# Distance attention: position products written to PSUM without gaps, and ACT's copies reading PSUM with a step

## The chip, the cores and the metric

The kernel runs on one core of a Trainium2 chip. The metric is the device time of one execution in microseconds (us). A core has five engines that run side by side and meet through semaphores: TensorE (PE in the profile; PEld is its weight load), VectorE (DVE), ScalarE (ACT), GpSimd (POOL) and SyncE (SP), which here issues DMAs. PE writes its results to PSUM; DVE and ACT read them from there.

## The reference

Four layers run one after the other on x of shape (8, 512, 128): a sine-weighted attention, a mixture of experts, distance attention, and a mixture of experts again. The change is in the third. Cut to that layer (16 heads of 8 values, sequence length 512, of which the positions' table is clamped at its ends):

```python
q, k, v = [(h @ W.T + b).reshape(B, S, 16, 8) for each of q, k, v]
scores = einsum('bqhd,bkhd->bhqk', q, k) / sqrt(8)           # content
pos_emb = dist_emb[MAX_POS - 1 + (pos_q[:, None] - pos_q[None, :])]
scores = scores + einsum('bqhd,qkd->bhqk', q, pos_emb)       # r1: the query with the distance
scores = scores + einsum('bkhd,qkd->bhqk', k, pos_emb)       # r2: the key with the distance
probs  = softmax(scores, axis=-1)
ctx    = einsum('bhqk,bkhd->bqhd', probs, v)
x      = x + ctx
```

## The kernel before

`distance_attention` works in 64 units. A unit u is one query block q of 128 positions of two batches (16 of them, 32 heads together, BH = 32) with one of QT = 4 key tiles of 128 positions. Four units, kt = 0 to 3, make a query block. The unit with kt = 0 of the next query block is the turn: in it the finished block is also transposed, exponentiated and multiplied with V.

One list `plan` sets the order of PE, ACT and DVE alike. A plain unit (kt = 1, 2, 3) is four steps "r1", four steps "r2", four steps "c". In the turn, 16 steps "e" (turn the scores), 8 steps "pv" (values) and 2 steps "o" (outputs) stand between them: r1 x4, r2 x2, e, e, r2, e, e, pv, r2, and so on.

Every step but "pv" fills a slot of `psR`, a ring of RING = 3 slots of two PSUM banks (1024 FP32 values per partition). A fill may start when the fill three places before it in the plan has been taken (`free_slot`): r1, r2 and e are taken by ACT, c and o by DVE.

- **Products** (`positions`, L1709): the position products of a step are 16 matmuls. Each loads a 112 x 128 window of the table `T` as weights, shifted by two positions from one matmul to the next, and moves 64 columns of `qb` (r1) or `kb` (r2): two positions n, 32 heads h. A bank takes 8 matmuls, so 16 positions of 32 heads.
- **Copies** (`keep`, L1785): ACT copies the 1024 values of a slot into `r1` or `r2` in SBUF, both laid out as [128, head, position].
- **Content** (`content`, L1721 and L1724): 8 matmuls of q with k for 8 heads, gapless output, then 8 transposes of `r1` that add to the same place. The first of a unit waits until ACT has copied the last r1 step.
- **Adds** (L1822): DVE adds the slot and `r2` into `S`. The first of a unit waits until ACT has copied the last r2 step. Then four maxima over `S` (L1830); in the turn also the maximum over the key tiles (L1834) and the subtraction for every head (L1837).
- **Spreading** (`spread`, L1655): POOL lays ks out as `kb` for every unit, and qs as `qb` once in a query block, in two copies each, after SP has loaded them (L1610). `load_k(u)` waits until the content of unit u - 2 is done. In the unit with kt = 2 POOL spreads ks, then qs for the next query block, and only then ks of the next unit.

Of the kernel before, what the change touches and what calls it, by code (L numbers as in the profile page):

```python
# [1510 lines left out]
def distance_attention(nc, sb, ps, sem, a, X, ident, dram):  # L1511
# [5 lines left out]
    BH = NB * H  # L1517
# [4 lines left out]
    CP = P // CH  # L1522
    HB = BH // 4
    NPAIR = BH // 2
    RING = 3
# [39 lines left out]
    with ExitStack() as c:  # L1565
# [15 lines left out]
        psR = ps(c, "psR", [P, RING, 2, L])  # L1581
# [11 lines left out]
        act_took = sem(c, "act_took")  # L1593
# [87 lines left out]
        def _(pe):  # L1681

            def free_slot(n):
                if n >= RING:
                    old = fills[n - RING]
                    if old in by_act:
                        pe.wait_ge(act_took, by_act[old])
                    else:
                        pe.wait_ge(dve_took, by_dve[old])
                return psR[:, n % RING, :, :]  # L1690

            def positions(kind, u, k):
                q, kt = divmod(u, QT)
                qt = q % QT
                if kind == "r1":
                    src, way, w0 = qb[:, q % 2, :, :, :], 1, L - 1 + P * kt - P * qt
                    if k == 0:
                        pe.wait_ge(qb_ready, 2 * (q + 1))
                else:
                    src, way, w0 = kb[:, u % 2, :, :, :], 0, L - 1 + P * qt - P * kt  # L1700
                    if k == 0:
                        pe.wait_ge(kb_ready, 2 * (u + 1))
                n = fill[kind, u, k]
                slot = free_slot(n)
                for j in range(CP // 2):
                    pair = k * (CP // 2) + j
                    w = w0 - 2 * pair
                    out = slot[:, j // 8, :].rearrange("p (h n) -> p n h", h=BH)
                    mm = pe.matmul(out[:, 2 * (j % 8):2 * (j % 8) + 2, :], T[:, way, w:w + P],  # L1709
                                   src[:, pair, :, :], start=(j % 8 == 0), stop=True,  # L1710
                                   skip_group_check=True)
                mm.then_inc(filled, 1)
# [51 lines left out]
            for kind, i, k in plan:  # L1764
                if kind in ("r1", "r2"):
                    positions(kind, i, k)
                elif kind == "c":
                    content(i, k)
                elif kind == "e":
                    turn(i, k)  # L1770
                elif kind == "pv":
                    values(i, k)
                else:
                    outputs(i, k)

        @block.scalar
        def _(act):

            def keep(kind, u, k):
                n = fill[kind, u, k]  # L1780
                act.wait_ge(filled, n + 1)
                if kind == "r2" and u:
                    act.wait_ge(dve_took, by_dve["c", u - 1, 3])
                dst = r1 if kind == "r1" else r2
                act.copy(dst[:, :, k * CP:(k + 1) * CP].rearrange("p h (a n) -> p a h n", a=2),  # L1785
                         psR[:, n % RING, :, :].rearrange("p a (h n) -> p a h n", h=BH)).then_inc(act_took, 1)

            def weigh(q, j):
                n = fill["e", q, j]
                act.wait_ge(filled, n + 1)  # L1790
                pair = q * NPAIR + j
                if pair >= RING_W:
                    act.wait_ge(pv, (pair - RING_W) // 2 + 1)
                act.activation(W[:, pair % RING_W, :, :].rearrange("p a n -> p (a n)"),  # L1794
                               psR[:, n % RING, :, :].rearrange("p a n -> p (a n)"),
                               ACT.Exp, scale=1.0 / SHARP).then_inc(act_took, 1)

            def take(q, i):
                if q or i:
                    act.wait_ge(filled, fill["o", q - (i == 0), 1 - i] + 1)  # L1800
                act.wait_ge(pv, q * NQUAD + (i + 1) * GPB)
                act.copy(oS[:], psO[:, i, :, :].rearrange("p g n -> p (g n)")).then_inc(o_taken, 1)

            for kind, i, k in plan:
                if kind in ("r1", "r2"):
                    keep(kind, i, k)
                elif kind == "e":
                    weigh(i, k)
                elif kind == "pv" and k % GPB == GPB - 1:
                    take(i, k // GPB)  # L1810
# [108 lines left out]
```

## Time and profile before

| | us |
|---|---|
| median of 3 runs | 4286.14 |
| lowest, highest | 4275.76, 4294.15 |
| the profiled execution | 4281.09 |
| its span, first to last instruction | 4279.3 |

A profile is one execution. Its span is 1.8 us shorter than that execution's time. Its page shows in 40 slices of 107 us how busy each engine was, and which share of its full clock PE was granted; there are two levels, 2.4 GHz (1.0) and 1.2 GHz (0.5), and a slice shows their mean. The timeline shows instructions in order of time, merged into groups; "idle before" is what the engine waited for. The ends of matmuls are modelled, their starts are recorded; a matmul lasts far longer than the distance to the next one's start, since they are pipelined. So the pace of PE is read from starts.

### The profile page before, as it was taken

To read this page: it belongs to the slowest core of one execution; us is meant where nothing else is said; L and a number is where in the kernel's file an instruction comes from. 1 tells how busy PE (TensorE), PEld (TensorE's weight loads), DVE (VectorE), ACT (ScalarE), POOL (GpSimd) and SP (SyncE) were. 2 spreads that over 40 slices of the span, in tenths; PEclk is the share of its full clock that TensorE was granted. 3 is DMA by queue.
4 is the path that set the end of the run, shared out by engine and by line. 5 is a ranking of instruction groups with operands and counts; after the bars stand their busy time and mean duration, and the time that the engine had idled before them with its cause. 6 is when DMAs were issued, how large, how long until landed. Compare 5 with 4: busy or idle time off the path is not lost. (4 is left out here: it accounts for less than half of the span.)

```text
span 4279.3 us, 71834 instructions
## 1 busy us (share of the span) xinstructions
PE 3602.2 (84%) x27092; PEld 2304.4 (54%) x27092; DVE 3409.0 (80%) x4519; ACT 2868.0 (67%) x2433; POOL 1271.6 (30%) x918
## 2 busy tenths in 40 slices
PE   3799999999999999999658814999999999998890
PEld 2233333333333333333347814989989889987690
DVE  6899999999999999999465544777777777776662
ACT  3899999999999999999323313555565565654430
POOL 2111111112112121212003343544544544531245
PEclk8899999999999999999869957999999999998895
DMA  5000000000000000000221227222223223312022
GB/s 141 17 12 6 12 12 12 6 12 12 12 9 9 12 12 12 6 12 9 99 71 36 61 65 164 54 47 59 55 45 59 55 45 59 61 31 80 20 64 67
DMA packets 149707, 174.78 MB, mean 41 GB/s; under 512 B 63824, under 2 KB 124848, under 8 KB 141264
## 3 DMA queue, kind: packets, MB, share of 16 engines
q1 hardware_dynamic: 140752, 153.35, 15.5%
q0 software_dynamic: 8704, 17.84, 1.8%
q8 instruction: 186, 3.05, 0.3%
q14 instruction: 65, 0.53, 0.0%
HBM read 119.04 MB, written 52.10 MB: 40 GB/s over the span
## 5 line engine op out<-in xcount | busy, mean ns | idle before, releaser
L704 PE MATMUL psA<-wave,diag 128*128 128x512 f32 x3072 | 1445.5, 622 | 136.5 <-DVE score L860 86.7
L772 ACT ACTIVATE wave<-wave 128x2048 f32<-128x2048 int32 x640 | 1181.2, 1904 | 3.6 <-DVE wave L847 2.2
L704 PEld LDWEIGHTS psA<-wave,diag 128*128 128x128 f32 x3072 | 584.4, 197 | 897.5 <-issue 699.2
L1785 ACT COPY r<-psR 128x1024 f32<-128x1024 f32 x512 | 482.6, 1039 | 358.1 <-PE psR L1709 357.5
L641 POOL TENSOR_TENSOR diag<-ident,par 128x128 f32<-128x128 f32 x384 | 292.6, 788 | 1441.0 <-PE psA L704 1441.0
L1655 POOL COPY kb<-ks 48x2048 bf16<-48x2048 bf16 x128 | 486.4, 3800 | 638.2 <-DMA ks<-kb_parts 534.5
L822 DVE TENSOR_SCALAR wave<-s,par 128x2048 int32<-128x2048 int32 x480 | 612.1, 1275 | 0.0
L847 DVE TENSOR_SCALAR wave<-wave 128x2048 int32<-128x2048 int32 x512 | 609.3, 1215 | 0.0
L1822 DVE TENSOR_TENSOR S<-psR,r 128x1024 f32<-128x1024 f32 x256 | 313.5, 1225 | 290.1 <-PE psR L1724 272.0
L737 ACT ACTIVATE s<-psS,par 128x1024 int32<-128x1024 f32 x256 | 282.8, 1105 | 132.4 <-PE psS L667 132.4
L1794 ACT ACTIVATE W<-psR 128x1024 f32<-128x1024 f32 x256 | 252.2, 1040 | 150.7 <-PE psR L1733 150.7
L860 DVE SCALAR_TENSOR_TENSOR score<-wave,par,psA 128x1024 f32<-128x1024 f32 x256 | 317.7, 1272 | 39.2 <-PE psA L704 39.2
L860 DVE SCALAR_TENSOR_TENSOR score<-wave,par,score 128x1024 f32<-128x1024 f32 x256 | 316.4, 1275 | 0.0
L1733 PE MATMUL psR<-ident,S 128*128 128x128 f32 x2048 | 269.5, 289 | 48.6 <-DVE S L1837 47.6
L1837 DVE TENSOR_SCALAR S<-S,m 128x512 f32<-128x512 f32 x512 | 307.8, 674 | 2.3
L1830 DVE TENSOR_REDUCE mx<-S 128x8 f32<-128x1024 f32 x256 | 297.8, 1210 | 0.0
L1709 PE MATMUL psR<-qb,T 112*128 112x64 bf16 x4096 | 244.5, 248 | 41.3 <-POOL qb L1655 41.3
L1733 PEld LDWEIGHTS psR<-ident,S 128*128 128x128 f32 x2048 | 241.5, 149 | 66.7 <-DVE S L1837 56.5
L1724 PE MATMUL psR<-ident,r 128*128 128x128 f32 x2048 | 266.8, 273 | 0.0
L1709 PEld LDWEIGHTS psR<-qb,T 112*128 112x128 bf16 x4096 | 237.0, 126 | 45.1 <-issue 42.1
L1709 PE MATMUL psR<-kb,T 112*128 112x64 bf16 x4096 | 245.8, 247 | 17.2 <-POOL kb L1655 17.2
L1709 PEld LDWEIGHTS psR<-kb,T 112*128 112x128 bf16 x4096 | 233.5, 125 | 23.3 <-POOL kb L1655 19.9
(254 smaller groups left out, 4473.7 us busy)
## 6 DMA issues: line engine op xcount, KB each, us to landing
ks<-kb_parts SPq DMA_DIRECT2D x128, 384.0 KB, 5.9
qs<-qb_parts SPq DMA_DIRECT2D x32, 384.0 KB, 8.5
ys<-f_ys SPq DMA_DIRECT2D x36, 256.0 KB
wave_out<-og SPq DMA_DIRECT2D x33, 256.0 KB, 2.1
o<-wave_out SPq DMA_DIRECT2D x8, 1024.0 KB, 5.1
qp<-qa_parts SPq DMA_DIRECT2D x32, 192.0 KB, 3.5
kp<-ka_parts SPq DMA_DIRECT2D x32, 192.0 KB, 4.0
f_wu<-in_w_up SPq DMA_DIRECT2D x2, 2048.0 KB, 10.4
```

The lines of the kernel that those rows point to most:

```text
L704: mm = pe.matmul(psA[:, kt, :], diag[:, h % 2, f, :], wave[:, h % 2, f, kt * L:(kt + 1) * L], start=(f == 0), stop=(f == PE_F - 1), skip_g ...
L772: act.activation(wave[:, h % 2, f, :], angle[:, h % 2, f, :], ACT.Sin, scale=float(TWO_PI / 2.0 ** 32)).then_inc(sine, 1)
L822: dve.tensor_scalar(angle[:, h % 2, f, :], src, scalar, par[:, u, row, h * NF + f:h * NF + f + 1], ALU.mult, ALU.add).then_inc(turned if f ...
L847: dve.tensor_scalar(angle[:, h % 2, f - 1, :], at, 32 - FRAC, None, ALU.logical_shift_left).then_inc(cut, 1)
L860: dve.scalar_tensor_tensor(out=score[:, u * HG + h, cols], in0=wave[:, h % 2, f, cols], scalar=par[:, u, 1, h * NF + f:h * NF + f + 1], in ...
L1655: pool.tensor_copy(dst[rows, :, odd, :], src[rows, :, :].rearrange("r h (n two) -> r n h two", two=2)[:, :, :, odd]).then_inc(ready, 1)
L1709: mm = pe.matmul(out[:, 2 * (j % 8):2 * (j % 8) + 2, :], T[:, way, w:w + P], src[:, pair, :, :], start=(j % 8 == 0), stop=True, skip_group ...
L1733: mm = pe.matmul(slot[:, i, kt * P:(kt + 1) * P], S[:, 2 * j + i, kt * P:(kt + 1) * P], ident[:], start=(kt == 0), stop=True, is_transpose ...
L1785: act.copy(dst[:, :, k * CP:(k + 1) * CP].rearrange("p h (a n) -> p a h n", a=2), psR[:, n % RING, :, :].rearrange("p a (h n) -> p a h n", ...
L1822: dve.tensor_tensor(S[:, hs, kt * P:(kt + 1) * P], psR[:, n % RING, :, :].rearrange("p a (h n) -> p (a h) n", n=P), r2[:, hs, :], ALU.add) ...
L1830: dve.tensor_reduce(mx[:, hs, kt], S[:, hs, kt * P:(kt + 1) * P], AX.X, ALU.max).then_inc(maxed, 1)
L1837: dve.tensor_scalar(S[:, h, :], S[:, h, :], m[:, h:h + 1], None, ALU.subtract).then_inc(shifted, 1)
```

## The change

Two access patterns change, and with them the place of each value inside a PSUM slot. Before, a bank held [head, position]: value (h, n) lay at 16 h + n, and the 64 results of a product went to 32 places 64 bytes apart, two neighbours each. Now a bank holds [position, head]: value (n, h) lies at 32 n + h, and the 64 results lie in one row. ACT read a slot in order and wrote to SBUF in runs of 16 values. Now it reads with a step of 32 values (128 bytes) through both banks, 32 positions for each head, and writes runs of 32. The values in `r1` and `r2` are the same. The number and order of instructions on every engine and all waits stay as they are.

```diff
-                    out = slot[:, j // 8, :].rearrange("p (h n) -> p n h", h=BH)
+                    out = slot[:, j // 8, :].rearrange("p (n h) -> p n h", h=BH)
                     mm = pe.matmul(out[:, 2 * (j % 8):2 * (j % 8) + 2, :], T[:, way, w:w + P],
                                    src[:, pair, :, :], start=(j % 8 == 0), stop=True,
                                    skip_group_check=True)
...
-                act.copy(dst[:, :, k * CP:(k + 1) * CP].rearrange("p h (a n) -> p a h n", a=2),
-                         psR[:, n % RING, :, :].rearrange("p a (h n) -> p a h n", h=BH)).then_inc(act_took, 1)
+                act.copy(dst[:, :, k * CP:(k + 1) * CP],
+                         psR[:, n % RING, :, :].rearrange("p a (n h) -> p h (a n)", h=BH)).then_inc(act_took, 1)
```

## Rows read from the trace of the kernel before

**Rows 1.** The page, part 2: PE's busy tenths and its clock, 40 slices.
```profile
PE   3799999999999999999658814999999999998890
...
PEclk8899999999999999999869957999999999998895
```
**Rows 2.** Timeline of a plain unit: start, us, engine, line, operation, [idle before <-releaser].
```profile
2912.01 3.74 PE L1709 MATMUL psR<-qb,T 112*128 112x64 bf16 x64
...
2913.10 7.43 ACT L1785 COPY r<-psR 128x1024 f32<-128x1024 f32 x8 [5.05 <-PE psR L1709]
...
2915.55 3.76 PE L1709 MATMUL psR<-kb,T 112*128 112x64 bf16 x64
...
2920.48 0.61 PE L1721 MATMUL psR<-ks,qs 112*128 112x128 bf16 x8
...
2920.68 5.20 DVE L1822 TENSOR_TENSOR S<-psR,r 128x1024 f32<-128x1024 f32 x4 [2.75 <-PE psR L1724]
...
2920.93 1.04 PE L1724 MATMUL psR<-ident,r 128*128 128x128 f32 x8
...
2924.46 3.74 PE L1709 MATMUL psR<-qb,T 112*128 112x64 bf16 x64
```
**Rows 3.** Instructions by line: duration in ns, min/median/max, first and last start.
```profile
L1709 PEld LDWEIGHTS psR<-kb,T x4096: 96/126/126, 2649.1 to 3887.2; 112*128 112x128 bf16 x196
...
L1785 ACT COPY r<-psR x512: 1012/1030/1094, 2643.7 to 3887.6; 128x1024 f32<-128x1024 f32 x171
...
L1655 POOL COPY kb<-ks x128: 3659/3810/3992, 2641.7 to 3878.7; 48x2048 bf16<-48x2048 bf16 x128
```
**Rows 4.** Timeline: first unit's start, POOL's copies, third unit, turn, next start.
```profile
2899.39 3.84 PE L1709 MATMUL psR<-qb,T 112*128 112x64 bf16 x63
...
2905.87 7.69 POOL L1655 COPY kb<-ks 48x2048 bf16<-48x2048 bf16 x2 [32.81 <-DMA ks<-kb_parts]
...
2929.08 3.75 PE L1709 MATMUL psR<-kb,T 112*128 112x64 bf16 x64 [0.88 <-POOL kb L1655]
...
2937.97 3.74 PE L1709 MATMUL psR<-qb,T 112*128 112x64 bf16 x64
...
2944.57 7.62 POOL L1655 COPY kb<-ks 48x2048 bf16<-48x2048 bf16 x2 [5.24 <-DMA ks<-kb_parts]
...
2945.42 9.43 DVE L1837 TENSOR_SCALAR S<-S,m 128x512 f32<-128x512 f32 x8
...
2952.53 1.97 PE L1733 MATMUL psR<-ident,S 128*128 128x128 f32 x16 [2.64 <-DVE S L1837]
...
2977.15 3.06 PE L1709 MATMUL psR<-qb,T 112*128 112x64 bf16 x49
```
**Rows 5.** Waits, 2641 to 3890 us: waiting <- awaited, us, times, longest.
```profile
PEld psR L1709 <- POOL kb L1655: 19.9, 16, 2.2
```
**Rows 6.** Instructions by line, as rows 3: DVE's reads of PSUM.
```profile
L977 DVE TENSOR_SCALAR orec<-psG x8: 224/225/226, 2102.0 to 2149.8; 128x64 f32<-128x64 f32 x8
L989 DVE TENSOR_TENSOR Y<-psY,bo x32: 278/280/293, 2107.2 to 2155.6; 128x128 f32 x32
L1329 DVE COPY f_ys<-f_pp x36: 678/681/692, 2321.7 to 4181.8; 128x512 f32<-128x512 f32 x36
```
**Rows 7.** Timeline: the r1 products of the first unit, at half clock.
```profile
2641.76 6.48 PE L1709 MATMUL psR<-qb,T 112*128 112x64 bf16 x64 [41.27 <-POOL qb L1655]
```
**Rows 8.** Stretches: length, busy us of the engines, PEclk, DMA share, GB/s.
```profile
2709.00:2712.40 3.40, 1.38 (x26) 1.06 (x18) 3.40 (x2) 1.78 (x2) 2.90 (x1) 1.00 0.00 0
2712.40:2715.80 3.40, 3.40 (x20) 3.07 (x23) 3.37 (x8) 1.03 (x1) 0.00 (x0) 0.50 0.00 0
...
2777.20:2819.50 42.30, 39.15 (x588) 35.15 (x586) 31.09 (x49) 24.13 (x26) 8.58 (x3) 0.92 0.21 39
2858.30:2899.50 41.20, 37.98 (x589) 34.69 (x587) 31.18 (x49) 24.13 (x26) 8.94 (x3) 0.96 0.21 40
2938.00:2977.20 39.20, 36.56 (x588) 33.27 (x586) 30.55 (x49) 24.02 (x26) 8.89 (x3) 1.00 0.21 42
```

## The prediction

> **What bounds the kernel now.** I read the page first for the stages [rows 1]. The change touches only distance attention, slices 25 to 37 of 40, 2641.8 to about 3893 us. There PE is busy in nine tenths of nearly every slice, at nine tenths of its clock. Busy shares don't say who sets the pace, so I went to the timeline of a plain unit [rows 2]. One (query block, key tile) unit is 12.45 us long, from PE's r1 products at 2912.01 to the next at 2924.46. PE has no gap: 64 r1 products (3.55 us), 64 r2 products (3.57), four content blocks of 1.33 each (5.3). ACT's eight copies begin 1.09 us after the first product and follow each other every 0.91 us ((7.43 - 1.03) / 7, with the 1.03 of one copy from rows 3). PE fills a slot in 16 x 56 ns = 0.90 us. So in the product phase PE and ACT have one pace; the content phase is PE's alone. DVE's first add waits for the last copy (2920.53, add at 2920.68).
>
> The third unit of each query block and the turn differ [rows 4]. POOL spreads ks(2), qs and ks(3) in one row, from 2905.87 until 2929.0, and PE's r2 products wait for it (0.88 us; there are 16 such waits, of 15 third units and the first unit of all, up to 2.2 us [rows 5]). In the turn, PE waits 2.64 us at 2952.53 for DVE's subtraction of the maximum. Eight of those subtractions take 9.43 us, and the wait ends when POOL's copy of 2944.57 to 2952.19 is over. Both waits belong to POOL and to the landing of ks, which this change doesn't touch.
>
> **Part 1: the products.** Each of 8192 products reads 64 columns and writes 64 values per partition, 64 bytes apart, two by two. They start 56 ns apart: 64 of them from 2912.01 to 2915.55 [rows 2]. The content matmuls, 128 columns with an equally large weight load and a gapless output, also start 56 ns apart: eight from 2920.48 to 2920.93. So a product takes as long as a matmul of twice its columns. Is that the strided write or the weight load? The load of a product takes 126 ns in the median but 96 at the least [rows 3]: most wait some 30 ns for something, and a load that finds the array free isn't the limit. That leaves the write, or a floor for changing weights. Bounds for the new interval: below, 27 ns (half of 55, the columns alone); above, 56 (no change). I take 30, near the lower end, since content shows that load and matmul overlap fully; at 40 the sum changes by 0.15 us a unit. A slot is then filled in 0.48 us.
>
> **Part 2: the copies.** 512 copies read 1024 values at 128-byte steps. No row shows ACT reading with a step. The nearest is DVE at L977, 64 values of PSUM at the same 128-byte step, 225 ns [rows 6]. Gapless reads of PSUM by DVE give (681 - 280) / (512 - 128) = 1.04 ns a value, so 64 would take 280 - 64 x 1.04 = 213. The step costs at most 12 ns on 64 values, 0.19 ns each; on a copy that is 0 to 0.2 us. I take 0. That the runs it writes get longer I cost at nothing: at 0.91 us for 1024 values ACT already takes 0.89 ns a value, less than the 1.04 of those gapless reads.
> The Trainium skill, "Advanced Engine Details and Errata", section Memory Cachelines, says that PSUM lines hold two FP32 values and that every two consecutive elements should be contiguous. That speaks for the faster product and against the copy; if it held for ACT's reads as for PE's writes, the third rival below would be the result. The DVE row doesn't bear it out for reads.
>
> **Part 3: a plain unit, step by step** (t from the first product). First copy at 0.48 + 0.2 = 0.70 instead of 0.90 + 0.2 = 1.09. Copies are then ACT's own, every 0.90. PE runs ahead, but the ring has three slots: content block 0 takes the slot of the sixth copy, free at 0.70 + 5 x 0.90 + 1.02 + 0.1 = 6.3. Then 5.3 of content: the unit is 11.64 instead of 12.45, 0.81 less. So of 128 x 26 ns = 3.3 us that PE saves, ACT's pace eats 2.5. DVE's adds fit in: the first waits for the eighth copy (8.2), later ones follow the content blocks, and the last ends 1.4 after the unit, as now (1.5).
>
> **Part 4: what POOL keeps.** From the start of the first unit after a turn (2899.39), POOL's row ends 29.7 us later whatever PE does: 6.5 until ks has landed, 23.2 for six copies [rows 4]. Units 1 and 2 gain 1.5 together, and PE only waits longer in unit 3: r1 is done 2.6 after its start at 23.6 (11.95, since the first of these units waits for DVE's adds, + 11.64), then PE idles some 3.5 us. From the end of that wait, the unit took 8.85 (3.57 + 5.3) and now takes 0.70 + 0.90 + 1.02 + 0.1 + 5.3 = 8.0. So a query block gains 0.85, not 2.4. In the turn, the end of POOL's copy sets when PE goes on, 14.6 us in; behind it PE has 24.6 us of work without a product in it. The turn gains the 0.1 of DVE's last add. Sum: 15 query blocks x 0.85 = 12.8, the last, without a qs to spread, 2.3, first unit 0.85 (its r2 waits for POOL too, rows 5), turns 1.5: **-17.4 us**.
>
> **Part 5: the clock.** PE's waits grow, and waits cost clock here [rows 8]. A stretch with 1.38 us of PE in 3.4 is followed by one at 0.50; the turn whose 2.6 us wait stands in rows 4 kept 1.00. The granted clock was 1.00 in that turn of 39.2 us, 0.96 in one of 41.2, 0.92 in one of 42.3; these three stand for the 15. Cut out the same way, 4 of the 15 turns are of the first kind, 6 of the second, 5 of the third (mean 41.0). With the new products the work ahead of the wait is done some 1.4 us sooner, so the wait becomes 4.0 us; I take no turn to keep the clock, 9 at 41.2 and 6 at 42.4, mean 41.7: **+11 us** (bounds 0 and +21, all at 42.4). In unit 3 the wait of 3.5 us is new: a stretch of 3.4 us at half clock behind it lies partly over products that ACT paces anyway and partly over content, where it costs up to 1.7. I take 0.6, the nearer end being that of the products: **+9** (bounds 0 and +26).
>
> Sum: -17.4 + 11 + 9 = +2.6. The profiled execution took 4281.1 us (span 4279.3), 5 below the median 4286.1 of the runs shown, so 4283.7 against the one and 4288.7 against the other: I say **4286**. This case alone spans 4264 (no cost of clock) to 4316 (both upper bounds).
>
> **Rivals.**
> 1. The interval stays at 56 ns, because changing weights has a floor and not the write. For it: at half clock the 64 first products took 6.48 us [rows 7] instead of 3.74, so the limit scales with PE's clock, as a floor in the array would. Against: content overlaps load and matmul in the same 56. Then nothing moves: 4281 to 4286.
> 2. Slower: PE's clock falls in the product phases of every unit, not only behind the long waits. Now PE has no gap there [rows 2]; after, it works 0.48 and waits 0.42 in each 0.90. Against it: the waits are short, and the turn of rows 4 kept its clock over one of 2.64. No row shows so fine a pattern of work and waits, and it decides as soon as the chip takes it as it took the waits of the other turns. Price: one stretch of 3.4 us at half clock on content in each of 64 units, 64 x 1.7 = 109, less the 17: 4373. The Trainium skill, "TensorE: Matmul & The Clock Gate", section HAM oscillation, tells of a kernel that loses the clock in every round to a wait; that is this rival's course.
> 3. Slower: ACT reads stepped values at half rate, a copy every 1.81 us. A unit is then 0.7 + 5 x 1.81 + 1.9 + 0.1 + 5.3 = 17.05, three of them 51.2 instead of 38.6, x 16 = +201; the turn resumes at 17.5 instead of 14.6, x 15 = +45: 4527. It decides from about 1.1 us a copy; below that POOL's waits hide it.
> 4. Faster: the clock holds in the waits and POOL's copies get shorter, toward their shortest, 3.66 instead of 3.81 [rows 3]: six in a row give 0.9 a query block, -14 beyond the -17: 4250.
>
> **Chances.** Forecast 0.53; rival 1 0.18; rival 2 0.10; rival 3 0.12; rival 4 0.07. A measurement of this kernel can tell about 0.5%, 21 us, from no change (4265 to 4308). The forecast lies inside that bound by 0.39, above it by 0.09, below by 0.05; rival 1 inside by 0.17, and 0.01 above. Faster 0.05 + 0.06 = 0.11; same 0.39 + 0.17 + 0.01 (rival 4) = 0.57; slower 0.09 + 0.01 + 0.10 + 0.12 = 0.32. The range leaves out rival 3, part of rival 4 and the end of rival 2: 4260 to 4360.
>
> **What would show each step.** Part 1: 64 products of r1 in about 2.5 us or ring-bound, weight loads near 98 ns in the median. Part 2: L1785 at 1.01 to 1.03 us, 0.90 apart. Part 3: plain units of 11.6. Part 4: r2 of the third unit still ending a wait for POOL, now about 3.5 us, the three units together 37.7 instead of 38.6. Part 5: 0.50 stretches behind the waits, about 15 and up to 15 more; PE's clock 1.00 in the product phases. The prediction is wrong if L1785 grows past 1.1 us, if the loads stay at 126, or if the mean clock of the stage falls below about 0.95.

## The result and the profile after

| | before | after |
|---|---|---|
| median, us (11 runs each) | 4283.54 | 4299.68 |
| lowest, highest | 4273.48, 4294.15 | 4289.86, 4308.77 |
| span of the profiled execution | 4279.3 | 4300.5 |

The ratio of after to before is 1.0037, with a 95% interval of 1.0024 to 1.0050: the change makes the kernel 16 us slower. The forecast was 4286, a step of +2.6. What moved is read in the order of the prediction.

**The products are twice as fast, the copies as fast as before.** By line (duration in ns, min/median/max, first and last start), as [rows 3]:

```profile
L1709 PEld LDWEIGHTS psR<-kb,T x4096: 96/99/134, 2654.4 to 3908.7; 112*128 112x128 bf16 x196
L1709 PE MATMUL psR<-kb,T x4096: 189/193/242, 2654.4 to 3908.7; 112*128 112x64 bf16 x196
L1785 ACT COPY r<-psR x512: 1012/1030/1099, 2648.0 to 3909.9; 128x1024 f32<-128x1024 f32 x171
```

The load of a product fell from 126 to 99 ns in the median, about what the content's loads take (98 ns, before and after). The copies kept 1012/1030, although each now reads PSUM with a step of 128 bytes.

**A plain unit, the third unit and the wait in the turn.** PE's timeline (start, us, ..., what it waited for), to be held against [rows 2] and [rows 4]:

```profile
2918.18 1.10 PE L1709 MATMUL psR<-qb,T 112*128 112x64 bf16 x32
2919.66 1.11 PE L1709 MATMUL psR<-qb,T 112*128 112x64 bf16 x32 [0.38 <-DVE S L1822]
2920.92 0.63 PE L1709 MATMUL psR<-kb,T 112*128 112x64 bf16 x16 [0.15 <-ACT r L1785]
2921.74 0.64 PE L1709 MATMUL psR<-kb,T 112*128 112x64 bf16 x16 [0.20 <-ACT r L1785]
2922.66 0.64 PE L1709 MATMUL psR<-kb,T 112*128 112x64 bf16 x16 [0.28 <-ACT r L1785]
...
2924.59 0.61 PE L1721 MATMUL psR<-ks,qs 112*128 112x128 bf16 x8 [0.36 <-ACT r L1785]
...
2929.89 1.10 PE L1709 MATMUL psR<-qb,T 112*128 112x64 bf16 x32
2931.38 1.11 PE L1709 MATMUL psR<-qb,T 112*128 112x64 bf16 x32 [0.39 <-DVE S L1822]
2935.98 3.48 PE L1709 MATMUL psR<-kb,T 112*128 112x64 bf16 x64 [3.50 <-POOL kb L1655]
2939.29 0.61 PE L1721 MATMUL psR<-ks,qs 112*128 112x128 bf16 x8
...
2944.60 1.10 PE L1709 MATMUL psR<-qb,T 112*128 112x64 bf16 x32
...
2954.84 0.64 PE L1709 MATMUL psR<-kb,T 112*128 112x64 bf16 x16
2959.67 3.61 PE L1733 MATMUL psR<-ident,S 128*128 128x128 f32 x16 [4.19 <-DVE S L1837]
```

Sixteen products take 0.63 us, of which the last one's own 0.19 is not interval: (0.63 - 0.19) / 15 = 29 ns between starts, where it was 56. But from 2921.74 on the slots follow each other at 0.92 us, ACT's pace, and PE waits 0.2 to 0.3 us for each. The unit is 2929.89 - 2918.18 = 11.71 us instead of 12.45. In the third unit PE now waits 3.50 us for POOL (2935.98; 3.67 in the mean of the 14 middle query blocks, where it was 1.05), and the next turn begins at 2944.60. In the turn it waits 4.19 us for the subtraction (2959.67); the longest wait of a turn is 3.85 us in the mean of the 15, where it was 2.93.

**The clock.** Stretches of this kernel (length, busy us of PE, PEld, DVE, ACT, POOL, PEclk, DMA share, GB/s). The first row is the second half of a turn and, from 2906.3 on, two plain units and a third unit up to the last 0.3 us of its wait. Then come 5.8 us of another third unit (r1 products and all but the last 0.6 us of the wait for POOL), and what follows them; then the wait in a turn, and what follows it:

```profile
2884.70:2935.70 51.00, 43.98 (x792) 40.01 (x792) 35.50 (x44) 29.59 (x32) 22.62 (x6) 1.00 0.25 48
2848.00:2853.80 5.80, 2.50 (x69) 2.25 (x67) 5.70 (x6) 3.76 (x4) 5.74 (x2) 1.00 0.63 137
2853.90:2860.70 6.80, 6.34 (x84) 6.28 (x85) 0.47 (x2) 3.76 (x4) 5.90 (x3) 0.50 0.02 4
2955.20:2959.60 4.40, 0.28 (x10) 0.16 (x6) 4.40 (x3) 1.27 (x2) 4.07 (x2) 1.00 0.00 0
2959.70:2963.10 3.40, 3.40 (x16) 3.24 (x16) 3.40 (x7) 1.03 (x1) 0.00 (x0) 0.50 0.02 5
```

And the same view over 1160 us of the stage, kernel before:

```profile
2680.00:3840.00 1160.00, 1098.71 (x16812) 1039.88 (x16811) 872.17 (x1087) 678.41 (x728) 556.00 (x147) 0.98 0.27 52
```

kernel after:

```profile
2680.00:3840.00 1160.00, 972.94 (x16592) 888.92 (x16592) 849.93 (x1052) 666.78 (x716) 553.06 (x146) 0.93 0.27 52
```

The time in it at half clock rose from 55 to 167 us, in 11 stretches before and 29 after. Before, all lay in turns (11 of the 15). After, over the whole layer, one begins in the wait for POOL, mostly near its end, in each of the 15 third units that have such a wait, and one lies in 14 of the 15 turns. In the product phases of the first and second units, with their waits of 0.2 to 0.4 us, the clock stayed at 1.00 in all query blocks but one. There ks had landed late, and PE waited 1.28 us for POOL in the second unit too; the clock fell behind that wait, and the unit took 12.60 us instead of 11.71:

```profile
3324.83 3.57 PE L1709 MATMUL psR<-kb,T 112*128 112x64 bf16 x64 [1.28 <-POOL kb L1655]
...
3324.90:3328.30 3.40, 3.40 (x65) 3.40 (x66) 2.00 (x2) 2.91 (x4) 3.40 (x1) 0.50 0.41 67
```

To see where the time went, the lengths of the units, from start to start of their r1 products, in us, as means over the 14 query blocks in the middle. All kernels of the experiments stand in it:

| | turn | first | second | third |
|---|---|---|---|---|
| before | 41.04 | 12.62 | 12.45 | 13.68 |
| after | 41.41 | 11.85 | 11.78 | 15.91 |
| fill3 | 41.66 | 11.85 | 11.71 | 14.44 |
| fill_both | 39.69 | 11.85 | 11.71 | 14.20 |
| qturn_before | 38.60 | 12.62 | 12.45 | 12.45 |
| qturn_after | 39.41 | 11.85 | 11.71 | 11.71 |
| poolturn_before | 36.59 | 12.62 | 12.45 | 12.45 |
| poolturn_after | 35.97 | 11.87 | 11.71 | 11.71 |
| act_only | 40.93 | 12.62 | 12.45 | 13.74 |
| step2 | 40.95 | 12.62 | 12.45 | 13.55 |
| pairs | 40.67 | 13.32 | 13.25 | 13.25 |
| read_step | 40.24 | 13.32 | 13.25 | 13.25 |
| pairs_write | 41.71 | 11.87 | 11.71 | 15.79 |

A query block of after is 80.95 us long, of before 79.79: 1.16 more, times 15 is 17 us. The first two units give 1.44 back, the third takes 2.23, the turn 0.37.

### The profile page after: what moved, and what is told of

Same layout as the page of the kernel before. It is cut to its first block and busy times, and to the rows that moved or that the text cites. A ratio compares the mean times of both kernels' runs of the same rounds, so it can differ in the third digit from the quotient of the medians.

```text
span 4300.5 us, 71834 instructions
## 1 busy us (share of the span) xinstructions
PE 3474.3 (81%) x27092; PEld 2148.8 (50%) x27092; DVE 3406.5 (79%) x4519; ACT 2867.9 (67%) x2433; POOL 1271.9 (30%) x918
## 5 line engine op out<-in xcount | busy, mean ns | idle before, releaser
L1724 PE MATMUL psR<-ident,r 128*128 128x128 f32 x2048 | 276.3, 279 | 0.0
L1709 PE MATMUL psR<-kb,T 112*128 112x64 bf16 x4096 | 180.4, 206 | 97.2 <-POOL kb L1655 62.6
L754 ACT ACTIVATE score<-score 128x2048 f32<-128x2048 f32 x132 | 241.4, 1899 | 6.1 <-DVE score L860 5.7
L679 PE MATMUL psO<-score,Vg 128*9 128x512 f32 x1056 | 239.8, 596 | 6.8 <-ACT score L754 6.8
L1724 PEld LDWEIGHTS psR<-ident,r 128*128 128x128 f32 x2048 | 228.9, 145 | 0.0
```

What stands on the lines that cost most here:

```text
L1724: mm = pe.matmul(slot[:, j, :], r1[:, k * HB + j, :], ident[:], start=False, stop=True, is_transpose=True, skip_group_check=True)
```

## Experiments

The theory: the 1.44 us that the first two units save in a query block are lost to POOL's row of copies in any case, and the time on top comes from half clock behind the two longer waits. The rivals: the new access patterns themselves cost something (ACT's stepped reads, or more traffic in the third unit), or the turn is what got slower for a reason of its own. Kernels that ran beside each other share the runs of before. These had medians of 4288.4, 4254.2 and 4254.5 us in the three groups, so times are compared within a group, and between groups by ratio alone.

### Filling the third unit's wait (fill3)

Kernel after, with 50 matmuls that nobody reads in place of part of PE's wait for POOL. What they write is overwritten by the products.

```diff
                     if k == 0:
+                        if kt == 3 and q < NQ - 1:
+                            busy = free_slot(fill[kind, u, k])
+                            for j in range(50):
+                                pe.matmul(busy[:, 0, 0:P], T[:, 0, 0:P], T[:, 0, P:2 * P],
+                                          start=True, stop=True, skip_group_check=True)
                         pe.wait_ge(kb_ready, 2 * (u + 1))
```

> The changed kernel, with 50 matmuls of 128 columns (56 ns each, 2.8 us) that PE does into the free slot while it waits for POOL's kb in the third unit of the first 15 query blocks. Their results are overwritten; every wait and every other instruction stays. Theory (the loss is the granted clock that falls behind that wait of 3.5 to 4.3 us): the third unit goes from 15.9 us to 13.7 to 14.2, units 1 and 2 stay at 11.85 and 11.71, the stretch at half clock around the third unit goes away, the turn stays at 41.4: 15 x 1.9 = 28 us less than the changed kernel, near 4271, ratio to the kernel before 0.997. Rival (the wait itself, or POOL's and the DMAs' pace, costs the time, and the clock is only seen beside it): the third unit stays at 15.9 and the time at 4300.

Measured: 4282.38 us (12 runs) beside 4288.41, ratio 0.9983 (0.9970 to 0.9996). PE's timeline in the third unit, the filler at L1705 and products now at L1714:

```profile
2852.34 2.97 PE L1705 MATMUL psR<-T 112*128 112x128 bf16 x50
2855.91 1.57 PE L1714 MATMUL psR<-kb,T 112*128 112x64 bf16 x48 [0.60 <-POOL kb L1655]
...
2858.65 0.61 PE L1726 MATMUL psR<-ks,qs 112*128 112x128 bf16 x8 [0.36 <-ACT r L1790]
```

The stretches around it, which answer to 2848.00 and 2853.90 of after:

```profile
2851.10:2855.90 4.80, 4.07 (x82) 3.78 (x82) 4.52 (x5) 3.02 (x4) 4.69 (x2) 1.00 0.74 143
2855.90:2863.90 8.00, 7.46 (x128) 7.22 (x129) 3.42 (x3) 3.76 (x4) 7.11 (x2) 1.00 0.01 3
```

PE is no earlier at its products: POOL's row ends 29.84 us after the first unit's start, against 29.89 in after and 29.86 in before (means). What changed is the time from there to the next turn: 8.16 us instead of 9.64 (before: 8.89), and 8.05 in most query blocks. So more work on PE makes this kernel 0.54% faster than after (1.0037 to 0.9983, across groups), some 23 us, and 15 times the third unit's 1.47 is 22. Neither ACT's reads nor PE's writes changed in it, so neither is the cause in the third unit. The third unit came out at 14.44 us, a little above the 13.7 to 14.2 expected: POOL's row ends 6.28 us into that unit, and 8.05 us follow even at full clock, 14.33 in all.

### Filling both waits (fill_both)

fill3, and 55 more ahead of the turn's long wait.

```diff
             def turn(q, j):
+                if j == 4 and q < NQ - 1:
+                    busy = free_slot(fill["e", q, j])
+                    for i in range(55):
+                        pe.matmul(busy[:, 0, 0:P], T[:, 0, 0:P], T[:, 0, P:2 * P],
+                                  start=True, stop=True, skip_group_check=True)
                 pe.wait_ge(shifted, q * BH + 2 * j + 2)
```

> The changed kernel with the 50 matmuls in the third unit's wait for POOL, and 55 more (3.1 us) that PE does in the turn's wait of 4.2 us for the stretched subtractions. POOL, DVE, ACT and all waits stay; only PE is kept at work in its two long waits. Theory: with the clock held in both, what is left is the sum of the prediction without its clock terms: third unit 14.1, turn 39.3 to 39.6, 17 us less than the kernel before would be with its own 0.50 stretches, and these (16 in its 15 turns, some 1.5 us each, 23 us) are gone too: 40 us less, ratio 0.991. Rival (part of the turn's 41.4 us isn't clock): the turn stays above 40.5 and the ratio at 0.997.

Measured: 4219.61 us (5 runs) beside 4254.53, ratio 0.9918 (0.9904 to 0.9932). The stage's stretch, as above:

```profile
2680.00:3840.00 1160.00, 1048.47 (x18936) 958.36 (x18933) 888.01 (x1109) 696.95 (x750) 567.16 (x149) 1.00 0.27 53
```

The clock never fell in these 1160 us. PE's time from the wait's end to the next turn is 8.05 in every query block, and the turn 39.69. Against after that is 1.71 + 1.71 a query block, 51 us in all, and the ratios differ by 1.19%, 51 us. These fillers also cure turns that were slow in before (mean 41.04, where one that kept its clock took 39.2, [rows 8]). So 0.9918 isn't what the change alone is worth at full clock; the kernel before with the same fillers wasn't run.

### Without POOL's row ahead of the third unit (qturn_before, qturn_after)

The spread of qs moves out of the row into the turn, behind the subtractions. Both kernels get the same edit:

```diff
                     load_k(u)
-                if u % QT == 1 and u // QT + 1 < NQ:
+                if u % QT == 0 and u // QT + 1 < NQ:
                     load_q(u // QT + 1)
...
                 spread_k(u)
-                if u % QT == 2 and u // QT + 1 < NQ:
+                if u % QT == 1 and u // QT + 1 < NQ:
+                    if u // QT:
+                        pool.wait_ge(shifted, u // QT * BH)
                     spread_q(u // QT + 1)
```

> The changed kernel, with POOL's spread of the next query block's qs moved out of the row ks(2), qs, ks(3) into the turn, behind DVE's subtractions; its load is issued one unit earlier. Theory: the third unit's wait for POOL is gone, so all three units are 11.7 to 11.85 and PE has no long wait in them: query block start to start 35.3 + 41.4 instead of 39.5 + 41.4, 15 x 4.2 = 63 us less than the changed kernel, near 4237. Rival 2 of the prediction (the clock falls in the product phases too) would show 0.50 in units without a long wait. Rival: the qs load lands beside ks of the turn and makes POOL's copy and DVE's stretched subtractions later: the turn grows by 1 to 3 us, 15 to 45 us back.

> The kernel before, with the same move of qs. Its third unit waits 1.1 us for POOL, so theory: 13.68 goes to 12.45, 15 x 1.2 = 18 us less, near 4265. So the change would be worth about 28 us (0.6 to 0.7%) where POOL doesn't hold the third unit, and costs 16 where it does. If the moved qs costs in the turn, both kernels with the move carry the same cost and their difference stands.

Measured, 5 runs each beside 4288.41: qturn_after 4212.36, ratio 0.9817 (0.9794 to 0.9839); qturn_before 4236.26, ratio 0.9868 (0.9845 to 0.9891). Between them lie 24 us, 0.5%: this is the change once POOL no longer holds the third unit. Three units then save 0.77 + 0.74 + 0.74 = 2.25 us, times 15 is 34, and the turn, 0.81 longer, takes 12 of them.

The move itself gained more than POOL's row: the turn fell by 2.0 us with the change and by 2.4 without it. DVE's 32 subtractions of a turn take as long as before (22.0 and 21.8 us), and two of them are still stretched by POOL's two copies of the next unit's ks. But these copies begin some 11.3 us into the turn and no longer 7.2, since the load of that ks is now issued right behind the load of qs. In qturn_after, one turn's start, its longest wait, and POOL's copies:

```profile
2847.93 1.10 PE L1711 MATMUL psR<-qb,T 112*128 112x64 bf16 x32
...
2859.16 7.68 POOL L1655 COPY kb<-ks 48x2048 bf16<-48x2048 bf16 x2 [8.00 <-DMA ks<-kb_parts]
...
2867.18 3.58 PE L1735 MATMUL psR<-ident,S 128*128 128x128 f32 x16 [2.71 <-DVE S L1839]
```

That is the rival's later copy, but it didn't lengthen the turn. The longest wait of PE in a turn fell from 3.85 to 2.58 us (from 2.93 to 1.74 without the change; means of 15 turns), and over all query blocks the time at half clock is 41 us in 11 stretches instead of 174 in 30 (14 in 4 instead of 55 in 11 without the change). Why the later collision leaves PE a shorter wait wasn't taken apart.

### The copies alone (act_only)

Before's products with after's copies, as an edit of the kernel after. It leaves the heads and positions of `r1` and `r2` mixed up, so its output isn't the layer's:

```diff
-                    out = slot[:, j // 8, :].rearrange("p (n h) -> p n h", h=BH)
+                    out = slot[:, j // 8, :].rearrange("p (h n) -> p n h", h=BH)
```

> The kernel before with ACT's new copies alone (products still written 64 bytes apart, so the heads and positions of r1 and r2 are mixed up). Theory (a step of 128 bytes costs ACT's reads nothing): L1785 stays at 1.03 us and 0.90 apart, product interval 56 ns, the time that of the kernel before. Rival: the copies get longer by up to 0.2 us while products are written with a step at the same time, two stepped users of PSUM.

Measured, one run: 4287.08 us beside 4288.41. The copies:

```profile
L1785 ACT COPY r<-psR x512: 1012/1032/1102, 2649.1 to 3892.8; 128x1024 f32<-128x1024 f32 x171
```

ACT's read with a step costs nothing that shows here (1032 ns against 1030), also apart from the new products.

### POOL out of the subtractions as well (poolturn_before, poolturn_after)

In qturn POOL still spreads ks of the next unit beside the subtractions. Here it waits for them with both; the load of qs is issued as in qturn:

```diff
                     load_k(u)
-                if u % QT == 1 and u // QT + 1 < NQ:
+                if u % QT == 0 and u // QT + 1 < NQ:
                     load_q(u // QT + 1)
...
             for u in range(NU):
+                if u % QT == 1 and u // QT:
+                    pool.wait_ge(shifted, u // QT * BH)
                 spread_k(u)
-                if u % QT == 2 and u // QT + 1 < NQ:
+                if u % QT == 1 and u // QT + 1 < NQ:
                     spread_q(u // QT + 1)
```

> The changed kernel with the move of qs as before, and with POOL's spread of the second unit's ks held back too until DVE's subtractions in the turn are done, so that POOL copies nothing while they run. Theory of the turn (PE's wait of 2.6 to 4 us there, and the half clock behind it, belong to POOL's copy that stretches two subtractions): no subtraction over 1 us, PE's wait in the turn gone or under 1 us, no 0.50 there, turn 39.4 to about 36, near 4160. Rival (the turn waits for DVE's chain anyway: four maxima and 32 subtractions are 18.5 us): the stretched subtractions go, but PE now waits for the unstretched chain several times and the turn gains under 1 us, 4200.

> The kernel before with both moves of POOL. With it the pair shows what the change is worth when no unit and no turn waits for POOL: three units x 16 x 0.75 = 36 us (0.9%), if the clock holds in both; near 4200.

Measured: poolturn_after 4122.37 us (5 runs) beside 4254.22, ratio 0.9692 (0.9669 to 0.9716). poolturn_before 4168.55 (4 runs), ratio 0.9791 (0.9760 to 0.9823). The subtractions by line, kernel after:

```profile
L1837 DVE TENSOR_SCALAR S<-S,m x512: 470/481/4068, 2706.9 to 3934.1; 128x512 f32<-128x512 f32 x171
```

poolturn_before:

```profile
L1839 DVE TENSOR_SCALAR S<-S,m x512: 476/481/488, 2686.4 to 3814.6; 128x512 f32<-128x512 f32 x171
```

All 512 are now short; in after two in each turn took over 1 us. A turn's 32 need 15.5 us of DVE instead of 22.0, and the turn is 35.97 us. A stretch of 1060 us of poolturn_after:

```profile
2680.00:3740.00 1060.00, 954.61 (x17269) 867.59 (x17266) 803.61 (x1103) 692.13 (x748) 558.97 (x146) 1.00 0.30 58
```

The clock holds, without a filler, but for one stretch of 3.4 us in the turn that begins at 2889.8, behind a wait of 1.96 us; poolturn_before has none between its first and its last unit. The change is worth 46 us here, 1.1%, 10 more than the 36 expected: the turn fell by 0.6 us with it as well. poolturn_after is 3.1% faster than the kernel before and, by the ratios, 3.4% faster than the kernel after. I had expected 4160, which against the 4288 of the group before is 0.970; as a ratio that held.

### What makes a product fast (step2, pairs, read_step, pairs_write)

The change makes the product's output gapless, which is several things at once. Four kernels take them apart, one run each; what counts is the interval, not the time.

step2, results 8 bytes apart, all inside one 256-byte piece:

```diff
-                    out = slot[:, j // 8, :].rearrange("p (h n) -> p n h", h=BH)
-                    mm = pe.matmul(out[:, 2 * (j % 8):2 * (j % 8) + 2, :], T[:, way, w:w + P],
+                    out = slot[:, j // 8, :].rearrange("p (j h n) -> p j n h", h=BH, n=2)
+                    mm = pe.matmul(out[:, j % 8, :, :], T[:, way, w:w + P],
```

pairs, columns moved in another order, so that two neighbours come one after the other, 64 bytes between pairs. The columns are now read in turn from two rows of `qb` or `kb` that lie 64 bytes apart, which is what "64 bytes apart" means for the reads below:

```diff
-                    mm = pe.matmul(out[:, 2 * (j % 8):2 * (j % 8) + 2, :], T[:, way, w:w + P],
-                                   src[:, pair, :, :], start=(j % 8 == 0), stop=True,
+                    mm = pe.matmul(out[:, :, 2 * (j % 8):2 * (j % 8) + 2], T[:, way, w:w + P],
+                                   src[:, pair, :, :].rearrange("p n h -> p h n"), start=(j % 8 == 0), stop=True,
```

read_step has step2's layout and pairs' order of reading: gapless output, columns read 64 bytes apart. pairs_write reads in order and writes pairs 128 bytes apart:

```diff
-                    out = slot[:, j // 8, :].rearrange("p (h n) -> p n h", h=BH)
-                    mm = pe.matmul(out[:, 2 * (j % 8):2 * (j % 8) + 2, :], T[:, way, w:w + P],
+                    out = slot[:, j // 8, :].rearrange("p (g n t) -> p n g t", n=16, t=2)
+                    mm = pe.matmul(out[:, 2 * (j % 8):2 * (j % 8) + 2, :, :], T[:, way, w:w + P],
```

(ACT's copies of step2, read_step and pairs_write read accordingly.)

> The changed kernel with the two positions of a product side by side: value (pair, head, position) at 64 pair + 2 head + position, so the 64 results fill the same gapless 256 bytes, but each goes 8 bytes from the one before it; ACT reads pairs, 256 bytes apart. If what counts is that two results in a row are neighbours: 56 ns, the time near the kernel before. If what counts is how far the step is, or how many places are touched: 29 ns, near the changed kernel.

> The kernel before with the 64 columns of each product moved in the order (head, position) instead of (position, head). The slot's layout and ACT's copies stay as before; the results now go to PSUM two neighbours at a time (8 bytes), 64 bytes to the next pair, and the moving operand is read 64 bytes apart. If it is single steps in PSUM that double a product's interval: 29 ns, units of 11.7 as in the changed kernel. If any gap in the row of 64 does, or if the stepped read of bf16 from SBUF costs as much: 56 ns and the time of the kernel before.

> Of the run in which products wrote two neighbours at a time and read their columns 64 bytes apart (62 ns), the reading alone: the 64 columns are moved in the order (head, position), 64 bytes apart, the 64 results lie in one gapless row, and ACT reads pairs of values 256 bytes apart. If the 62 ns came from the stepped read of bf16: 62 ns here too, plain units of 13.25. If they came from the 8-byte pairs in PSUM: 29 ns, units of 11.7.

> The writing alone: the 64 columns are read gapless, and results go to PSUM two neighbours at a time, 128 bytes to the next two (the slot holds head pair, position, head in the pair). If two neighbours are enough for PSUM: 29 ns and units of 11.7, as in the changed kernel. If any gap costs: 56 ns.

| | results of a product | columns read | interval, ns | us |
|---|---|---|---|---|
| before | single, 64 bytes apart | in order | 56 | |
| step2 | single, 8 bytes apart | in order | 56 | 4257.70 |
| pairs | pairs, 64 bytes apart | 64 bytes apart | 62 | 4275.79 |
| read_step | gapless | 64 bytes apart | 62 | 4262.62 |
| pairs_write | pairs, 128 bytes apart | in order | 29 | 4272.53 |
| after | gapless | in order | 29 | |

step2's timeline, one unit's r1 and r2 and the next r1, 3.55 us for 64 products:

```profile
2742.51 3.74 PE L1709 MATMUL psR<-qb,T 112*128 112x64 bf16 x64
2746.06 3.77 PE L1709 MATMUL psR<-kb,T 112*128 112x64 bf16 x64
2754.97 3.74 PE L1709 MATMUL psR<-qb,T 112*128 112x64 bf16 x64
```

read_step's, 3.98 us for 64:

```profile
2740.40 4.14 PE L1709 MATMUL psR<-qb,T 112*128 112x64 bf16 x64
2744.38 4.13 PE L1709 MATMUL psR<-kb,T 112*128 112x64 bf16 x64
```

and a later unit of it, at full clock in its r1 products and at half clock in its r2 products:

```profile
2806.31 4.20 PE L1709 MATMUL psR<-qb,T 112*128 112x64 bf16 x64
2810.35 4.13 PE L1709 MATMUL psR<-kb,T 112*128 112x64 bf16 x64
...
2806.30:2810.50 4.20, 4.20 (x69) 4.12 (x68) 4.13 (x7) 2.95 (x3) 0.00 (x0) 1.00 0.89 172
2810.50:2813.90 3.40, 3.40 (x59) 3.40 (x57) 2.12 (x2) 3.40 (x5) 1.08 (x1) 0.50 0.17 24
```

pairs_write's third unit, with after's wait and after's slow row behind it:

```profile
2833.92 1.11 PE L1709 MATMUL psR<-qb,T 112*128 112x64 bf16 x32 [0.39 <-DVE S L1822]
2838.43 3.60 PE L1709 MATMUL psR<-kb,T 112*128 112x64 bf16 x64 [3.39 <-POOL kb L1655]
```

Neighbours in a row are what counts: single results cost 56 ns at 8 bytes as at 64, pairs cost 29 even at 128. The run pairs couldn't show that by itself, since its reading order costs 62 ns, with pairs as with a gapless row. read_step and pairs_write settled that. The 62 ns don't come from PE's clock either: the r2 products of the last rows take no longer at half clock than the r1 products at full clock. And the clock fell there while PE had no gap at all, in the first unit after a turn (five times in read_step, four in pairs), so half clock doesn't come behind waits alone. pairs_write reaches after's pace with another layout and shows after's third unit too (15.79 us), at a clock of 0.93 over the stage, as after: the loss comes with the faster product, not with the layout.

## Why the prediction was wrong

- **Part 1, products: right.** 30 ns taken, 29 measured. The write was the limit, not a floor for changing weights, so rival 1 fell. (Its evidence, that the time of a product scales with PE's clock, holds for the fast product too: 29 ns, and 52 at half clock.) The Trainium skill ("Advanced Engine Details and Errata", Memory Cachelines) asks for every two consecutive elements to be contiguous in PSUM. step2 (56) and pairs_write (29) agree for PE's writes. Its sentence that any pattern with gaps slows matmuls down a lot isn't borne out: pairs 128 bytes apart cost nothing.
- **Part 2, copies: right.** 0 taken, 0 measured (after, act_only). Rival 3 fell: ACT's reads 128 bytes apart paid nothing for having no neighbours in a row.
- **Part 3, plain unit: right but for 0.07.** 11.64 against 11.71.
- **Part 4, what POOL keeps: right, but for the first unit of all.** POOL's row ends 29.89 us after the first unit's start (29.7 given), PE waits 3.67 in the mean (3.5), and from there to the next turn a query block that keeps its clock takes 8.05 in fill3 and fill_both (8.0); none of after's kept it. At full clock the three units are 29.89 + 8.05 = 37.94 us instead of 38.75, a gain of 0.81 (0.85). The first unit of all, which was to gain 0.85, went from 16.25 to 16.86 us: it begins at half clock, and that lasted until 12.3 us into it, where it was 5.8 before.
- **Part 5, the clock in the turn: a little high.** +0.7 less 0.1 taken, +0.37 measured: 5.6 us in all instead of 9.5.
- **Part 5, the clock in the third unit: this step failed.** The prediction had the mechanism. It took the stretch at half clock to last 3.4 us, with a cost between 0 and 1.7, and chose 0.6, "the nearer end being that of the products", since ACT paces the products anyway. Measured: 9.64 - 8.05 = 1.59 us a query block, 24 us in all instead of 9. For the products the 0.6 was right: from the wait's end to the content it is 2939.29 - 2935.98 = 3.31 us at half clock, in which PE itself sets the pace with 52 ns a product, against 2858.65 - 2855.91 = 2.74 in fill3 at full clock. That block lost 0.57 in all (8.62 instead of 8.05). But that is the cost of a stretch of 3.4 us, and only 2 of the 15 third units had one so short. In the other 13 the half clock lasted 6.8 us, as in the one at 2853.90, and covered content as well, where PE alone sets the pace. These cost 1.78 us in the mean and up to 2.07 (10.12 - 8.05), so the mean lies at the upper bound and single blocks beyond it. What was wrong is the length of the stretch: [rows 8] has turns with either length (PEclk 0.96 over 41.2 us and 0.92 over 42.3), and the term for the third unit took the shorter one for all. Why it was the longer one in 13 of 15, no run shows.

With the measured terms in its own sum: -17.4 + 1.5 (the turn's gain in it) + 5.6 + 24 = +13.7. Measured were +16. In the profiled execution 1.5 of the rest is the first unit of all (0.60 lost instead of 0.85 gained), and 0.9 the second unit that lost its clock behind a wait of 1.28 us. Rival 2 had the right sign but the wrong place: the clock fell behind the waits for POOL and DVE, and in the product phases of the first and second units only that once in 32. The pattern of 0.6 us work and 0.3 us wait, which no row of before showed, cost no clock by itself. Rival 4's shorter POOL copies didn't come.

So the change does what it says, and pays only where somebody lets PE use it: +16 us here, -24 with POOL's row gone, -46 with POOL out of the subtractions too. Still open is why 14 of the 15 turns of after lose clock and only 11 of before, with longest waits of 3.85 and 2.93 us in the mean. The runs show that filling the waits ends it, not where the border lies: waits of 0.77 to 2.05 us in before's third units cost no clock; one of 2.32 us in a third unit of act_only did, and one of 1.28 in a second unit of after.

## What to carry to other kernels

Before making an engine faster, find the wait that ends last on it. If another engine holds that wait, the gain turns into idle time there, and on PE idle time can cost more than it saved: here over 110 us more at half clock, for products that saved 1.44 us per query block. Remove the holder first; here moving POOL's copies out of the way was worth more than the change ever was (2.1%, poolturn_before), and made the change worth 46 us where it had cost 16. When a term of the sum has two bounds and the clock is in it, work out who sets the pace at half clock, and take the length of the stretch from all rows that show one, before choosing between them.

## What the runs showed of the hardware

- A product of 64 columns with its 112 x 128 weights starts every 29 ns if each two results in a row are neighbours in PSUM, every 56 ns if they aren't, at 8 bytes apart as at 64 (step2, before). At half clock the fast one took 52 ns.
- Reading the moving bf16 columns in turn from two rows 64 bytes apart costs 62 ns a product, with pairs (pairs) and with gapless output (read_step), and no more at half clock.
- ACT copies 1024 FP32 values from PSUM to SBUF in 1.03 us, read in order or 128 bytes apart.
- A subtraction of 0.48 us on DVE took up to 4.07 us beside POOL's copies (3.8 us each), and 0.49 at most in poolturn_before, where none ran beside it. The Trainium skill ("SBUF — State Buffer", SBUF: two separate sides) says that GpSimd and some of DVE's instructions share a pair of ports as a lock, and that who comes second waits for the whole of the other's instruction. The rows agree: 4.07 is 0.48 and nearly one copy, and two such subtractions are about the 6.5 us that poolturn took out of each turn.
- 105 matmuls per query block that nobody reads, put where PE waited, made the kernel after some 51 us faster, with the clock at 1.00 over the 1160 us shown.
